# Six vector loads move from SyncE to ScalarE, and one pair's context goes ahead of its queries

## The reference

```python
def xattn(query, key_in, value, Wq, bq, Wk, bk, Wv, bv, gamma, beta):
    q = einsum('bsd,df->bsf', query, Wq) + bq
    k = einsum('bsd,df->bsf', key_in, Wk) + bk
    v = einsum('bsd,df->bsf', value, Wv) + bv
    probs = softmax(einsum('bqd,bkd->bqk', q, k))
    x = einsum('bqk,bkd->bqd', probs, v) + query
    return layernorm(x) * gamma + beta

x = x + xattn(layernorm(x), ctx_1024, ctx_1024, ...)   # x 32x64x256, ctx 32x1601x256
x = x + attn(layernorm(x), w_kv, w_q, b_q, w_out, b_out)
x = x + ffn(layernorm(x), router_w, router_bias, ...)  # 16 experts, top 2, and a shared one
```

## Time and profile before

| | us |
|---|---|
| median of three runs | 536.94 |
| the profiled execution | 534.44 |
| its span, first to last instruction | 532.3 |
| TensorE busy in it | 494.5 (93%) |
| VectorE busy | 386.8 (73%) |
| ScalarE busy | 219.3 (41%) |
| GpSimd busy | 203.7 (38%) |
| mean granted TensorE clock | 0.984 of 2.4 GHz |
| DMA, mean over the span | 205 GB/s |

### The profile page before, as it was taken

The page is one execution under the profiler, slowest core; times in us unless marked ns, Lnnn a source line. Parts: engine busy times, 40 slices in busy tenths (PEclk is TensorE's granted clock), DMA queues, the critical chain, the costliest instruction groups (busy, mean ns, idle before and its releaser), DMA issues.

```text
span 532.3 us, 14494 instructions
## 1 busy us (share of the span) xinstructions
PE 494.5 (93%) x5028; PEld 345.4 (65%) x5029; DVE 386.8 (73%) x1053; ACT 219.3 (41%) x656; POOL 203.7 (38%) x344
## 2 busy tenths in 40 slices
PE   7999969999999999999989999999998979999990
PEld 6866536665666656666655667766654548888870
DVE  4897489999789978898743478898766605555764
ACT  3444404533334444344432356666540025555520
POOL 5002130312211221222221476776776625665550
PEclk9999979999999999999999999999999989999997
DMA  8986968686998878885303899720022235555748
GB/s 290 377 313 175 364 195 279 194 265 227 339 299 298 285 232 270 277 273 204 112 21 107 245 309 325 238 90 1 33 75 86 90 109 150 155 158 141 239 100 246
DMA packets 67610, 108.92 MB, mean 205 GB/s; under 512 B 8371, under 2 KB 49381, under 8 KB 67560
## 3 DMA queue, kind: packets, MB, share of 16 engines
q1 hardware_dynamic: 60872, 97.57, 58.1%
q0 software_dynamic: 3792, 8.43, 4.5%
q10 hardware_dynamic: 2896, 2.23, 1.3%
HBM read 85.31 MB, written 24.85 MB: 207 GB/s over the span
## 4 chain that ended last, share of the span: by engine, by line
PE 71%; DMA 9%; DVE 6%; POOL 5%; issue 3%; SPq 2%; ACT 2%; ACTq 1%; POOLq 0%; DVEq 0%
PE banks L1206 15%; PE banks L1180 15%; PE banks L1590 8%; POOL rows_by_expert L773 4%; PE banks L1602 4%; PE banks L1194 3%; PE banks L1219 3%; DMA ring<-in_ctx_dram 3%; PE banks L1584 2%; DMA bk_col<-in_L_xattn_bk_dram 2%; PE banks L1317 2%; PE banks L1369 2%; PE banks L1227 2%; PE banks L1324 2%; PE banks L1340 1%
## 5 line engine op out<-in xcount | busy, mean ns | idle before, releaser
L1714 DVE STREAM_TRANSPOSE ctxT<-ring 128x832 f32<-128x832 f32 x124 | 118.2, 1009 | 8.8 <-DMA ring<-in_ctx_dram 8.5
L1180 PE MATMUL banks<-ctxT,qT_all 32*64 32x416 f32 (+2 forms) x2048 | 96.3, 507 | 6.3 <-DVE ctxT L1714 4.7
L1206 PE MATMUL banks<-ring,prob 128*64 128x256 f32 (+1 forms) x832 | 93.6, 381 | 0.7 <-ACT prob L888 0.7
L1180 PEld LDWEIGHTS banks<-ctxT,qT_all 32*64 32x64 f32 x2048 | 56.4, 133 | 37.0 <-issue 13.1
L1206 PEld LDWEIGHTS banks<-ring,prob 128*64 128x64 f32 (+1 forms) x832 | 58.6, 137 | 31.5 <-issue 4.2
L672 POOL TENSOR_TENSOR var<-mv,eps 128x1 f32<-128x1 f32 x32 | 6.2, 193 | 151.6 <-DVE mv L1755 97.1
L807 POOL DMA_INDIRECT expert_out<-prob,dest x47 | 46.3, 985 | 39.6 <-issue 21.6
L1590 PE MATMUL banks<-ring,ctxT 128*128 x188 | 49.4, 386 | 0.0
L901 ACT ACTIVATE prob<-banks,negmax 128x416 f32<-128x416 f32 (+2 forms) x80 | 41.0, 532 | 19.5 <-DVE negmax L1736 19.5
L1726 DVE TENSOR_REDUCE blockmax<-banks 128x1 f32<-128x416 f32 (+1 forms) x64 | 32.3, 566 | 20.5 <-PE banks L1180 20.5
L720 POOL TENSOR_TENSOR ctxT<-ctxT,k_mask 128x1088 f32<-128x1088 f32 x16 | 33.1, 2069 | 24.9 <-ACT ctxT L997 24.9
(11 more groups left out here) (279 smaller groups left out, 957.0 us busy)
## 6 DMA issues: line engine op xcount, KB each, us to landing
ring<-in_ctx_dram SPq DMA_DIRECT2D x48, 1024.0 KB, 8.5
qT_all<-q_by_pair SPq DMA_DIRECT2D x56, 128.0 KB, 8.0
rows_by_expert<-blank SPq DMA_DIRECT2D x8, 774.0 KB, 6.8
ctxT<-rows_by_expert SPq DMA_DIRECT2D x47, 129.0 KB, 2.1
mid<-stage SPq DMA_DIRECT2D x30, 128.0 KB, 2.3
ring<-in_ctx_dram SPq DMA_DIRECT2D x16, 130.0 KB
ctxT<-mid SPq DMA_DIRECT2D x16, 128.0 KB, 3.8
qT_all<-mid SPq DMA_DIRECT2D x16, 128.0 KB, 4.5
```

What stands on the lines that cost most here:

```text
L1180: last = pe.matmul(S[a][64 * b:64 * b + 64, 0:KW[a]], q_rep[mine, r, c, 64 * b:64 * b + 64], ctxT[mine, c, b, 0:KW[a]], start=c == 0, stop ...
L1206: last = pe.matmul(U[64 * b:64 * b + 64, 0:D], probT[0:rows, k, 64 * b:64 * b + 64], ring[0:rows, r, b, k, :], start=k == 0, stop=k == KT)
L1714: dve.transpose(ctxT[:, c].rearrange("p b (k j) -> p (b k) j", j=Q), ring[:, r].rearrange("p b k c -> p (b k) c")[:, :, columns(c):columns ...
```

## The change

SyncE no longer issues the six vector loads. ScalarE does, on its own queue, behind the copies of pair 0's probabilities and ahead of the exponentials of pair 1. And `follow` for pair 3 now issues the context first and the queries behind it, as pair 4's already did; `late` now names which semaphore of the query stores is waited for ahead of those query loads. Pair 4 stays as it was.

```diff
@@ SyncE
             store_q(0, DIRECT)
             sp.wait_ge(q_stored[0], 16 * QUADS)
             load_q(DIRECT, DIRECT)
-            for to, of in ((bv_b, "L0_xattn_bv"), (gamma_b, "L0_xattn_gamma"), (beta_b, "L0_xattn_beta")):
-                sp.dma_start(to[:, :], t[of].partition_broadcast(P)).then_inc(weights_loaded, 16)
-            sp.dma_start(bq2_col[:, :], t["L0_attn_b_q"].rearrange("(p a) -> p a", a=1)).then_inc(weights_loaded, 16)
-            sp.dma_start(bout_b[:, :], t["L0_attn_b_out"].partition_broadcast(P)).then_inc(weights_loaded, 16)
-            sp.dma_start(rbias_b[:, :], t["L0_ffn_router_bias"].partition_broadcast(P)).then_inc(weights_loaded, 16)
-            def follow(i, r, stores=True, late=False):
+            def follow(i, r, stores=True, late=None):
 
                 sp.wait_ge(block_used, (i - RING + 1) * BLOCKS)
-                if not late:
+                if late is None:
                     load_q(i, r)
                 if stores:
                     store(i - RING - 2)
                 for g in range(len(KPARTS)):
                     sp.wait_ge(pv_done, (i - RING) * len(KPARTS) + (g + 1))
                     load_part(i, r, g)
-                if late:
-                    sp.wait_ge(q_stored[1], 16 * QUADS)
+                if late is not None:
+                    sp.wait_ge(q_stored[late], 16 * QUADS)
                     load_q(i, r)
 
-            follow(RING, 0, stores=False)
-            follow(RING + 1, 1, stores=False, late=True)
+            follow(RING, 0, stores=False, late=0)
+            follow(RING + 1, 1, stores=False, late=1)
@@ ScalarE
             turned_out(0)
+            for to, of in ((bv_b, "L0_xattn_bv"), (gamma_b, "L0_xattn_gamma"), (beta_b, "L0_xattn_beta")):
+                act.dma_start(to[:, :], t[of].partition_broadcast(P)).then_inc(weights_loaded, 16)
+            act.dma_start(bq2_col[:, :], t["L0_attn_b_q"].rearrange("(p a) -> p a", a=1)).then_inc(weights_loaded, 16)
+            act.dma_start(bout_b[:, :], t["L0_attn_b_out"].partition_broadcast(P)).then_inc(weights_loaded, 16)
+            act.dma_start(rbias_b[:, :], t["L0_ffn_router_bias"].partition_broadcast(P)).then_inc(weights_loaded, 16)
             exps(1)
```

## The result

| | us |
|---|---|
| median of 20 runs, the change | 532.95 |
| median of 20 runs, the kernel before | 536.58 |
| ratio | 0.9944, 95% interval 0.9925 to 0.9963 |
| profiled execution, the change | 531.87 (span 529.7) |

By the ratio the kernel is faster by 3.0 us (2.0 to 4.0), by the medians by 3.6, where 7.1 were forecast. The ratio leaves out one run of the change (537.12), whose time was over 1.5% above the fastest. The direction was right and the size was not: under 1%, and about half of the sum or less.

The account below looks back on a forecast made before the run. The kernel was taken as bound by TensorE's chain, with an avoidable wait at pair 3's scores; -7.1 and +0 on the profiled 534.44 gave 527.3, or 529.8 us against the median 536.94; range 526.3 to 535.5.

Parts of the forecast that it names:

- The wait at pair 3: Pair 3's scores: 7.1 us lost, 4.7 by TensorE standing still and 2.3 by the slow clock, all to be won.
- The vectors beside the store: Vector loads moved beside SyncE's query store: pair 2's queries delayed by 1 to 2.5 us.
- The bound of 3.4: Upper bound on the store's delay: all 3.4 us of the vectors' DMA time ahead of it.
- The stall that I put at 0: TensorE's wait for pair 2's queries before its scores: 0, bounds 0 to 0.9 us.
- the latest that I gave: Latest start of pair 3's context load on SyncE's queue: 43.9 us.
- VectorE's room: How late pair 3's context may land without stopping TensorE's scores: 57.4 us.
- the step that failed: Pair 5's context, 1.8 us late against the shift, covered by VectorE's early blocks: cost 0, at most 1.8 us.
- my 77.1: Forecast issue time of pair 5's context on SyncE's queue, behind eight query loads and a store: about 77.1 us.
- The wait for the second store, which I had left at 72.34: Store on ScalarE that pair 4's queries wait for: said not to move, those queries still at 72.34 us.
- rival (c): Given back later: pair 4 or 5 lands late after all; gain about 5 us, 532 us, chance 0.12.
- The rival of ScalarE being held in its issues: Six issues ahead of pair 1's exponentials take over 7.7 us; up to 10.7 us slower, 547.6 us, chance 0.05.

Follow-up runs that it names:

- e8: The kernel before, unchanged, profiled once more and not timed; span 533.0 us.
- e2: The new order of pair 3 alone, with the six vectors still issued by SyncE where they were, against the kernel before; ratio 1.0009.
- e3: The change, but SyncE issues the six vectors between pair 3's context and its queries; ratio 0.9924 to the kernel before.
- e5: The change with SyncE issuing the vectors between pair 3's context and queries, and pair 5's queries behind its context; ratio 0.9903 to the kernel before.
- e6: As e5, but ScalarE issues the six vectors, behind the copies of pair 1's probabilities; ratio 0.9891 to the kernel before.
- e9: As e6, but pair 3's queries go ahead of its context again; ratio 0.9907 to the kernel before.
- e10: As e6, but pair 5's queries go ahead of its context again; ratio 0.9910 to the kernel before.
- e1: The change, but pair 3's queries go ahead of its context again, vectors still on ScalarE; ratio 0.9951 to the kernel before.
- e4: The change, with pair 5's queries also behind its context; ratio 0.9911 to the kernel before.
- e11: The changed kernel, unaltered, profiled once more and not timed; span 528.6 us.
- e7: The change, with four of the vector loads issued twice by ScalarE, first into unused memory; ratio 1.0030 to the kernel before.

## Why the prediction was wrong

**The wait at pair 3: mechanism right, size too large.** I took "7.1 us are lost here" from one profile. It was the one with the earliest start: in thirteen profiles of this case the weighing of pair 0 starts between 37.5 and 39.4 us. The edit can't be the reason: pair 1's scores, which stand ahead of it and run through, start at 31.73 before and at 32.91 after, and the first of the moved loads is issued at 33.02. In the kernel before, the context's landing hangs on the DMA queue and not on TensorE, so an early start is only waited away: TensorE started 1.7 us later in e8, VectorE began pair 3 only 0.9 later (63.40 for 62.54), the slow clock took 0.4 less, and pair 4's scores come at 87.75 against 87.44. Its loss was 5.8. The changed kernel, with the wait gone, pays its own start in full: the +1.2 of the table. A gain that is read as the length of a wait holds only if what comes before the wait starts as early next time.

**The vectors beside the store: right, near the upper bound.** I took a delay of 1 to 2.5 us. From the end of the store's last issue to the next row of SyncE's queue it took 6.1 us before; in the other seven profiles that have no vectors beside it 5.4 to 6.3 (e2, e3, e5, e6, e8, e9, e10), and with them 8.6 (after), 8.6 (e1), 8.0 (e4), 7.9 (e11). On average that is 8.3 against 6.1, so some 2.2 us are shown to be the vectors'. The bound of 3.4, all of the vectors ahead of the store, was not reached. The stall that I put at 0, bounds 0 to 0.9, was 0.6 in one profile of the change and nothing in the other (pair 2's scores start 9.8 and 9.2 us after pair 0's weighing, 9.2 before). The profile puts those 0.59 us down to ScalarE's copies, but in the profile before the scores start while the same copies still run; the last load of pair 2's queries, issued at 45.8, landed 2.5 us later, at 48.3, just ahead of the scores at 48.48. In the first profile the context is issued 2.5 us later than the latest that I gave: SyncE was through with its store's issues 1.3 us later than before, and its four query loads took 2.74 instead of 1.73 us. It still came inside VectorE's room as far as that had moved with the late start, and 0.2 us were lost.

The Trainium skill ("DMA: Bandwidth & Descriptors", Queues, rings and completion order, Arbitration) says that an engine takes turns between queues. These runs agree: the vectors on the other queue delay the store by some 2.2 us though they were issued beside and behind it, and in e7 twice as many delay what comes next.

**Pair 5: the step that failed.** This is the largest term that was wrong. I wrote "I cost it at 0, at most 1.8", trusting VectorE's early blocks. They do run ahead, but the last three blocks come behind them and behind VectorE's small work, and it is for these that TensorE stood. Measured: 2.5 and 1.7 us lost in the two profiles of the change, 1.9 in e3, 0.7 in e10, 0 in e4, e5, e6 and e9, whose only common edit puts pair 5's queries behind its context. The context also went later than my 77.1, at 80.74 and 79.72. The wait for the second store, which I had left at 72.34, ended at 74.73 and 74.21 (74.22 in e8, so that is not the change's doing alone), and SyncE's eight query loads took 4.3 to 4.8 us behind it, and not 3.60. This was rival (c), and its price of 2 us was about right.

**The sum.** Over the two profiles of each kernel, up to the end of pair 5's scores: 6.4 us for the wait at pair 3 (7.1 and 5.8), less 0.4 for the starts (38.8 against 38.4 on average), 0.3 at pair 2, 0.3 on the way through pair 3, 2.1 at pair 5: 3.3. That this is so near the 3.0 (2.0 to 4.0) of the timed runs is partly luck. Behind pair 5 two differences follow that nobody forecast, and they nearly cancel. At pair 15's weighing the change is 4.6 us ahead (266.2 for 270.8), 1.4 of it from the stretch between the weighings of pairs 8 and 9; from there to the end it takes 1.1 us longer (263.0 for 261.9), which leaves the 3.5 by which the spans differ.

**The new order of pair 3 is worth nothing measurable in this change.** e2 has it alone and gains nothing, e1 lacks it and is as fast as the whole. In e9 against e6, with vectors beside the context, the trace shows 2.8 us more between the weighings of pair 0 and 15 (228.8 against 226.1), the times no difference.

**What stays open.** Why e1's pair 5 lost only 0.2 us, with its queries first as in the change, is half settled. Against e3, which lost 1.9 with its context issued within 0.2 us of e1's, TensorE came to pair 5 0.9 us later (99.75 for 98.90) and VectorE could start 0.9 sooner (91.54 for 92.45); why the context landed sooner is not known. The stretch between the weighings of pairs 8 and 9 takes 14.4 us in four profiles (both of the change, e3, e9) and 15.3 to 15.9 in the other nine; no run shows what makes the difference, and it takes back much of what e4 to e6 win at pair 5. From pair 15's weighing to the end it takes 260.6 to 266.1 us, a spread as large as the effects here; the two profiles of one kernel differ there by only 0.6 and 0.2, so whether it is chance is open too. The rival of ScalarE being held in its issues did not come: 2.8 us for six, and 5.8 for ten in e7, inside the 7.7 us for which it waits anyway.

## What to carry to other kernels

When a wait goes, everything ahead of it counts again: take its length from more than one profile, at the latest start and not at the earliest. A load that is moved to another engine's queue is not moved away; look at which transfer that someone waits for is in flight at the new place, and put it where there is none (e10 is the change with the six loads one pair later on ScalarE: a gain of 4.8 us for 3.0, with intervals that overlap). And follow a shift to the next fixed point, here a second store and the eight loads that are queued behind it. A sum that agrees with the measured time should be checked at several stations on the way: here it agreed at pair 5 and at the end, and not in between.

## What the runs showed of the hardware

The granted clock and idle time of TensorE. After a gap of 1.84 us it stayed at 1.00:

```profile
104.00:106.00 2.00, 0.16 (x12) 0.14 (x16) 2.00 (x5) 0.00 (x0) 0.00 (x0) 1.00 1.06 394
106.00:108.00 2.00, 2.00 (x40) 0.57 (x45) 2.00 (x3) 0.00 (x0) 0.00 (x0) 1.00 0.93 260
```

(windows of the profile after, columns as in the earlier trace rows). It stayed at 1.00 after gaps of 1.05 us (e11), 1.25 (e3) and 2.26 (e7, at pair 5) as well. In e7, after 4.19 us idle at pair 2, it is 0.50 until 56 us, and 1.00 over 58 to 60:

```profile
54.00:56.00 2.00, 2.00 (x32) 1.12 (x24) 0.00 (x0) 0.00 (x0) 0.00 (x0) 0.50 1.00 399
56.00:58.00 2.00, 2.00 (x48) 1.48 (x40) 0.00 (x0) 0.00 (x0) 0.00 (x0) 0.81 1.05 416
58.00:60.00 2.00, 2.00 (x56) 1.26 (x46) 0.00 (x0) 0.00 (x0) 0.00 (x0) 1.00 1.06 256
```

But the 1.86 us of e9 were followed by a clock of 0.62 over 72 to 74 us and 0.53 over 74 to 76, and its 48 matmuls took 3.87 us, against 2.78 after the gaps of the change and e3. So the length of a gap alone does not say whether the clock falls, and a gap that is only shortened may keep its whole penalty: e2's was 2.95 us for 4.73, and its 48 matmuls took 4.44 us as before.

The six vector loads carry 0.52 MB, 1.4 us at the 369 GB/s of the earlier trace rows, and hold up others for longer: some 2.2 us for the store, and 3.6 us for pair 3's context, which landed 15.5 us after its first issue behind them and 11.9 in e1, where only they were gone.
